# Attention: how the softmax shift rows are turned, and which score bank a maximum takes

## The reference

```
q = (x @ Wq.T + bq).reshape(b, l, H, HD).transpose(0, 2, 1, 3)
k = (x @ Wk.T + bk).reshape(b, l, H, HD).transpose(0, 2, 1, 3)
...
q = _apply_rope(q, cos, sin)
k = _apply_rope(k, cos, sin)
scores = jnp.einsum('bhsd,bhed->bhse', q, k) * scale
attn = jax.nn.softmax(scores, axis=-1)
out = jnp.einsum('bhse,bhed->bhsd', attn, v)
```

## Time and profile before

| | |
|---|---|
| time of the runs | 1195.78 us median of 3 (1195.12 to 1197.62) |
| the profiled execution | span 1191.5 us; its own whole time is not recorded |
| around the span, by the median | 4.3 us |
| TensorE busy | 1039.4 us, 87% |
| VectorE busy | 853.0 us, 72% |
| ScalarE busy | 798.2 us, 67% |
| GpSimd busy | 291.2 us, 24% |
| granted TensorE clock | 0.934 on average, 1.00 between 450 and 1020 us |

### The profile page before, as it was taken

One profiled execution on the slowest core, in us unless ns is written; L12 is line 12 of the kernel. 1 busy time (PEld: TensorE's weight loads), 2 busy tenths in 40 slices (PEclk: granted clock), 3 DMA queues, 4 the chain that ended last, 5 costly groups with the idle time before them and its releaser, 6 DMA issues.

```text
span 1191.5 us, 22203 instructions
## 1 busy us (share of the span) xinstructions
PE 1039.4 (87%) x8296; PEld 485.1 (41%) x8300; DVE 853.0 (72%) x1585; ACT 798.2 (67%) x1206; POOL 291.2 (24%) x296
## 2 busy tenths in 40 slices
PE   9936767787989689999999999999999999968795
PEld 6512224786964222222222222222222222448694
DVE  2499997347135689999999999999999992362222
ACT  2653333455545469999999999999999999431122
POOL 0069881655334500000000000000000000026652
PEclk7969998889888879999999999999999999988997
DMA  3056530866642310011100111001110100038683
GB/s 104 1 166 195 179 122 36 260 189 201 186 136 88 122 61 25 12 34 34 34 16 20 34 34 34 9 27 34 34 34 2 33 4 4 4 126 266 204 268 124
DMA packets 49110, 104.16 MB, mean 87 GB/s; under 512 B 9440, under 2 KB 11864, under 8 KB 48620
## 3 DMA queue, kind: packets, MB, share of 16 engines
q1 hardware_dynamic: 43386, 91.76, 24.6%
q0 software_dynamic: 4544, 9.32, 2.4%
q10 hardware_dynamic: 1074, 1.67, 0.4%
HBM read 89.35 MB, written 12.94 MB: 86 GB/s over the span
## 4 chain that ended last, share of the span: by engine, by line
PE 61%; issue 12%; DVE 9%; ACT 9%; DMA 4%; POOL 2%; another core or an unknown queue 1%; SPq 1%; ACTq 0%; DVEq 0%; POOLq 0%
PE psum L966 19%; PE psum L945 12%; PE psum L956 8%; PE psum L1085 6%; PE psum L1096 6%; ACT probs L1339 5%; DVE tile_max L2044 2%; DVE ssm_h L1764 1%; PE psum L789 1%; PE psum L1068 1%; PE psum L769 1%; DMA y_in<-y_dram 1%; ACT ln_xn L1331 1%; POOL h0T L1483 1%
## 5 line engine op out<-in xcount | busy, mean ns | idle before, releaser
L1339 ACT ACTIVATE probs<-psum 128x1024 f32<-128x1024 f32 x512 | 504.2, 1041 | 27.6 <-PE psum L956 22.3
L2044 DVE TENSOR_REDUCE tile_max<-psum 128x1 f32<-128x512 f32 x720 | 459.8, 685 | 31.8 <-PE psum L945 25.1
L945 PE MATMUL psum<-k_stack,q_stack 62*128 62x512 bf16 x994 | 313.3, 388 | 14.1 <-DMA q_stack<-q_dram 8.6
L966 PE MATMUL psum<-probs,v_head 128*32 128x256 f32 (+1 forms) x3840 | 321.0, 406 | 0.6 <-ACT probs L1339 0.4
L956 PE MATMUL psum<-q_stack,k_stack 64*128 64x512 bf16 x1024 | 290.0, 384 | 10.6 <-ACT probs L1339 8.7
L945 PEld LDWEIGHTS psum<-k_stack,q_stack 62*128 62x128 bf16 x994 | 77.4, 94 | 242.7 <-issue 109.7
L966 PEld LDWEIGHTS psum<-probs,v_head 128*32 128x32 f32 x3840 | 75.7, 108 | 164.6 <-issue 126.0
L1535 POOL TENSOR_TENSOR max_parts<-row_max,no_shift 128x8 bf16<-128x8 f32 x32 | 6.4, 200 | 557.0 <-DVE row_max L2020 557.0
L1096 PE MATMUL psum<-w2r,hid 128*128 128x128 f32 x624 | 92.5, 296 | 25.4 <-issue 25.2
L1085 PE MATMUL psum<-x_cols,w1r 128*128 128x128 f32 (+1 forms) x624 | 93.5, 299 | 8.8 <-issue 8.0
L1096 PEld LDWEIGHTS psum<-w2r,hid 128*128 128x128 f32 x624 | 84.3, 210 | 28.0 <-issue 27.6
(11 more groups left out here) (287 smaller groups left out, 1107.5 us busy)
## 6 DMA issues: line engine op xcount, KB each, us to landing
w1r<-w SPq DMA_DIRECT2D x78, 256.0 KB
w2r<-w SPq DMA_DIRECT2D x78, 256.0 KB
ssm_b<-bc_dram SPq DMA_DIRECT2D x32, 512.0 KB, 4.0
k_stack<-k_dram SPq DMA_DIRECT2D x60, 120.0 KB
y_in<-y_dram SPq DMA_DIRECT2D x16, 256.0 KB, 5.1
q_stack<-q_dram SPq DMA_DIRECT2D x30, 96.0 KB
bc_p<-bc_dram SPq DMA_DIRECT2D x5, 512.0 KB, 5.7
xtok_dram<-x_tok SPq DMA_DIRECT2D x8, 256.0 KB, 2.4
```

The source lines that it names most:

```text
L945: mm(bank, queries, k_stack[rows, u, keys:keys + C], start=True, stop=True).then_inc(s1_ps, 1)
L966: i = mm(psum[32 * j:32 * j + VM, 7, lo:hi], v_head[:, u, kt, :], probs[:, kt % 4, j * C + lo:j * C + hi], start=kt == 0, stop=kt == KT - ...
L1339: f(probs[:, kt % 4, hf * HALF:(hf + 1) * HALF], banks(2 * slot, 2), ACT.Exp, scale=SCALE).then_inc(p_ready, 1)
L2044: v.tensor_reduce(top, bank, AX.X, ALU.max).then_inc(s1_read, 1)
```

## The change

Part one: `row` leaves TensorE and ScalarE. `max_parts` becomes a view of `max_squares`, 32 columns for each half of which 16 are used and the rest cleared once by GpSimd. VectorE turns it in four squares of 32 partitions by 32 columns, from partitions 0, 32, 64 and 96 into `shift_rows` at partition 0 (`turn_maxima`). The turn of a half stands after VectorE's maximum 36 of the same head and after maximum 2 of the next one (`TURN_AFTER`). The row loads wait for the squares. A head has 32 entries, and the slots alternate by half tile throughout. Part two: `bank_of` takes the head itself, not its number in the ring of four stacks.

```
-WIDES = [3, 9]
-PADS = 6
+WIDES = [3, 10]
+PADS = 7
...
-ROWS_AFTER = (8, 14)
-FIRST_ROW = SN // 2 + 12
+TURN_AFTER = (SN // 2 + 4, 2)
...
+SQUARE = 32
 ROW_LOADS = 16 * 2
+SQUARES = 128 // SQUARE
...
-    return 4 + (hs % UN + p) % RING if hs else FIRST_BANKS[p % len(FIRST_BANKS)]
+    return 4 + (hs + p) % RING if hs else FIRST_BANKS[p % len(FIRST_BANKS)]
...
-ENTRIES = 2 * KT + 2
-def entry(kt, hf, rows=True):
-    return 2 * kt + hf + (rows and sum(kt > after for after in ROWS_AFTER))
-ROW = [entry(after, 1) + 1 for after in ROWS_AFTER]
+ENTRIES = 2 * KT
+def entry(kt, hf):
+    return 2 * kt + hf
...
-        max_parts = sb("max_parts", [128, 2, 2, SHIFT, TPC], BF16)
+        max_squares = sb("max_squares", [128, 2, SQUARE], BF16)
+        max_parts = max_squares[:, :, 0:ROWS].rearrange("p h (d s j) -> p h d s j", d=2, s=SHIFT)
...
-        def load_rows(eng, h, u, hf, done):
-            eng.wait_ge(p_ready, done)
+        def load_rows(eng, h, u, hf):
+
+            eng.wait_ge(max_turned, SQUARES * (2 * h + hf + 1))
...
-                        if following and kt in ROWS_AFTER:
-                            hf = ROWS_AFTER.index(kt)
-                            row(h + 1, hf, h * ENTRIES + (2 + ROW[hf]), ROW[hf] % 2)
...
+                g.memset(max_squares[:], 0.0).then_inc(pool_made, 1)
...
-                        pool.wait_ge(s2_ps, hs * ENTRIES + (2 - ENTRIES))
+                        pool.wait_ge(max_turned, SQUARES * (n - 2))
...
+                def turn_maxima(hs, hf):
+                    dve.wait_ge(max_parts_ready, hs * 4 + (hf * 2 + 4))
+                    if hs:
+                        dve.wait_ge(rows_in[hf], hs * ROW_LOADS)
+                    for g in range(SQUARES):
+                        at = slice(SQUARE * g, SQUARE * (g + 1))
+                        v.transpose(shift_rows[0:SQUARE, hf, at], max_squares[at, hf, :]).then_inc(max_turned, 1)
...
+                        if p == TURN_AFTER[0]:
+                            turn_maxima(hs, 0)
+                        if p == TURN_AFTER[1] and hs:
+                            turn_maxima(hs - 1, 1)
...
+                turn_maxima(NH - 1, 1)
```

More of the change, by code:

```diff
@@ L509, in build @@
         apart_step, above_ready = sem("apart_step"), sem("above_ready")
-        row_max_ready, max_hi_ready, max_parts_ready = (sem(n) for n in ("row_max_ready", "max_hi_ready", "max_parts_ready"))
+        row_max_ready, max_parts_ready = sem("row_max_ready"), sem("max_parts_ready")
+        max_turned = sem("max_turned")
         rows_in = [sem(f"rows_in{hf}") for hf in range(2)]
@@ L669, in attention @@
                 load_k(sp, 1, 1)
[L670 removed]
+                load_rows(sp, 0, 0, 0)
                 load_q(sp, 2, 2)
@@ L945, in maxima @@
                     mm(bank, queries, k_stack[rows, u, keys:keys + C], start=True, stop=True).then_inc(s1_ps, 1)
[L947 to L952, removed]
                 def scores(u, kt, hf, slot, side):
@@ L957, in scores, with values @@
                               q_stack[rows, u, hf * C:(hf + 1) * C], start=True, stop=True)
-                def values(h, u, kt, rows, part=None):
+                def values(h, u, kt, part=None):
                     if kt == 0:
@@ L962, in values @@
                         pe.wait_ge(o_copied, h + 1)
-                    pe.wait_ge(p_ready, h * ENTRIES + (entry(kt, 1, rows) + 5))
+                    pe.wait_ge(p_ready, h * ENTRIES + (entry(kt, 1) + 3))
                     lo, hi = (0, C) if part is None else (part * C // 2, (part + 1) * C // 2)
@@ L1009, in attention @@
                         pe.wait_ge(v_all_ready, TILES)
-                    if p == FIRST_ROW:
-                        row(0, 0, 0, 0)
                     maxima(0, 0, p)
-                for p in range(RING):
-                    maxima(1, 1, p)
-                row(0, 1, 1, 1)
-                for p in range(RING, 2 * LEAD):
+                for p in range(2 * LEAD):
                     maxima(1, 1, p)
@@ L1316, in attention @@
                 first_q(act, 0, (0,))
-                def row(hs, hf, g, slot):
-                    act.wait_ge(s2_ps, g + 1)
-                    if hs:
-                        act.wait_ge(rows_in[hf], hs * ROW_LOADS)
-                    f(shift_rows[0:ROWS, hf, :], psum[0:ROWS, 2 * slot, 0:128], ACT.Identity).then_inc(p_ready, 1)
                 def above(hs, p):
@@ L1352, in attention @@
                 above(1, 0)
-                row(0, 1, 1, 1)
-                load_rows(act, 0, 0, 1, 4)
+                load_rows(act, 0, 0, 1)
                 for h in range(NH):
-                    following = h + 1 < NH
                     for kt in range(KT):
@@ L1361, in attention @@
                         for hf in range(2):
-                            exponentials(h, kt, hf, following)
+                            exponentials(h, kt, hf)
                         if kt == 0 and h:
                             keep(h - 1)
-                        if following and kt in ROWS_AFTER:
-                            hf = ROWS_AFTER.index(kt)
-                            row(h + 1, hf, h * ENTRIES + (2 + ROW[hf]), ROW[hf] % 2)
                 keep(NH - 1)
```

38 lines of the change are left out of this document (19 added, 19 removed).

## The result

The changed kernel takes 1196.37 us (median of 20 runs) against 1190.68 us of the kernel before (20 runs beside them): ratio 1.0049, 95% interval 1.0031 to 1.0067. By this ratio it is **slower by half a per cent, 5.8 us** (3.7 to 8.0), where 0.8 us less was forecast. Its profiled execution spans 1192.3 us.

A forecast was written before the change was run, and what follows sets the result against it. TensorE was taken to set the pace, VectorE and ScalarE close behind. Terms -20.4 - 2.7 + 20.6 + 1.7 = -0.8 us, added to 1195.78, gave 1195.0 us; own range 1192 to 1198.5, whole range 1184 to 1200.

The forecast's parts named there:

- What bounds the kernel, and no slack at the joined maximum: TensorE sets the pace; a VectorE delay before the joined maximum reaches it whole, rests of 0.25 us a block recover afterwards.
- Rows out: Heads 0 to 14: two rows each leave TensorE and ScalarE, 30 x 0.68 = -20.4 us.
- the rotation: Bank clash at the ends of heads 3, 7 and 11 disappears: 3 x 0.90 = -2.7 us.
- The turns on VectorE: Four squares before a joined maximum, 29 turns on the path at 0.71 us: +20.6 us, bounds 10.4 and 27.8.
- rival B: At the joined maximum behind each turn: squares dearer than 0.19 us, TensorE waits for VectorE; 1202.6 us at upper bound, chance 0.13.
- The sum with that estimate: Whole-kernel total if each VectorE square takes the 211 ns estimated from the skill's transpose figure: 1197.9 us.
- The start: Head 0's first rows: VectorE waits for GpSimd's parts, rows issue at 427.90 instead of 426.23: +1.7 us.
- Row DMAs in time: Row loads behind VectorE's count in SP's queue still arrive before the scores; slack 0.66 us in an ordinary head, no cost.
- A (squares overlap): In each VectorE turn squares overlap, a turn is 0.36 us and the joined maximum keeps its overlap; 1184.2 us, chance 0.27.
- C: Rows miss a head's second half tile and TensorE waits once a head, 3 us per 0.2 missed; 1198.0 us, chance 0.05.
- D: The 0.68 us stall behind a row is VectorE's rest, so removing rows wins nothing; 1215.4 us, chance 0.02.
- Edits costed at nothing: GpSimd's extra memset of 64 columns, 0.06 us covered by its wait, and row DMAs unchanged in number and queue place.

The follow-up runs named there:

- the first experiment: Changed kernel with four more squares behind each turn's four, all reading partitions 0 to 31: a head takes 38.66 us, against 37.89 in the changed kernel.
- the addition later: Changed kernel with GpSimd's bias addition to xT moved behind head 0's parts, removing VectorE's wait: start 22.37 us, against 27.14 in the changed kernel.
- all four edits: Changed kernel with one instruction a turn, first turn behind maximum 41, bias addition behind head 0's parts, head 0's row loads first on SP: ratio 0.9766 to before.
- the five runs: Five timed runs of the kernel with all four edits: median 1162.73 us, ratio 0.9766 (0.9741 to 0.979) to the kernel before.
- the single run: The earlier, single execution of the kernel with all four edits: 1168.04 us beside 1192.14.

## Why the prediction was wrong

Between the forecast of 0.8 us less and the 7.7 more of the two traces lie 8.5 us: 5.9 in the turns, 2.2 in the start, 0.45 at the last head. That 1196.37 us is close to the forecast of 1195.0 is luck: the 1195.78 of three runs it was added to lies 5.1 above the median of all 20 (1190.68), and the change was put 6.5 too low (by the medians). The 4.3 us around the span were too much as well; every run with both figures has 1.8 to 1.9 (1194.07 - 1192.3).

*What bounds the kernel, and no slack at the joined maximum.* Right. A turn of 0.82 to the reduce and 0.06 of lost overlap make 0.88, and TensorE loses 0.92; the 0.04 between I can't place. Nothing of the turn was taken up. Spread over rests, half of it was.

*Rows out, -20.4, and the rotation, -2.7.* The rotation is shown by itself, 2.77. The rows' 0.68 was not measured by itself, but what rests on it agrees: 0.915 a turn from the head against 0.92 from TensorE's two half tiles, and the 3.86 us from the first rows to the last copy.

*The turns on VectorE, +20.6: this step failed, in size.* The mechanism was the one taken: the squares and the joined maximum are held, shown by the four squares from one quadrant, which were not. But I let each square begin when the one before it ends and gave it the 0.18 of a 128x32 instruction; it lasts 0.20, and a held one begins 0.03 after that end: 0.23, three times. The last square's distance to the reduce, put at 0.09, is 0.82 - 3 x 0.23 = 0.13, and what a turn makes TensorE lose is 0.92. Turn 0.915, not 0.71: 26.5 us, not 20.6, near the upper bound of 27.8 worked out from two instructions in which one waits for the other, 0.22. Those rows were the nearer ones: a held square starts 0.23 behind the one before it, about as an instruction that waits for its forerunner, not 0.18 or 0.09 like one that merely follows it. By this rival B holds, with its condition (a turn above 0.74, heads over 37.8) met and a chance of 0.13 given. What it gave as a reason, that a square must be filled before it is emptied, is not what the turn paid for: squares of one quadrant start 0.10 apart.

The Trainium skill (page VectorE: DVE Perf Modes, section Two Vector instructions with no wait between them) named the held ones rightly: the second to fourth square and the joined maximum behind, in the changed kernel; the first of the four more, but not its followers, in the first experiment. Its word on when a held one starts is that every earlier one has finished; here that is the end shown in the trace and 0.03 to 0.04 more. The Trainium skill (same page, section The three transpose paths) led to an estimate of 211 ns a square, and the trace has 0.20. The sum with that estimate, 2.1 us more than before (1197.9), has the right sign and is nearer to the 5.8 measured than the forecast's 0.8 less.

*The start, +1.7: too low, 3.87.* Row_max was forecast 0.95 later and came 1.59 later: the turn took 0.93 where 0.63 was put in, and the 14 joined maxima (420.46 - 411.50 = 8.96) 0.64 each instead of 0.61. The issue is 2.44 later, forecast 1.67. The last 1.43 was not in the sum at all: I kept the landing of the row load at its old length. The landing varies: it took 6.16 to 7.12 us in the runs of VectorE's turns with the loads of heads 2 and 3 where the changed kernel has them, and 5.69 in the kernel before (5.96 with the rotation alone). With SP's loads of heads 2 and 3 held it was 5.05, with both row loads ahead of them on SP at most 3.3. Taking away the wait or the long landing, either alone, wins the start back: without the wait it is 22.37, with the rows first 23.18, before 23.27.

*Row DMAs in time.* Right in the ordinary heads, which all last the same. Not in the last one, where TensorE waits 0.36 for them and some 0.45 us is lost. The last turn was left out of the sum because VectorE has nothing else to do there, but its rows are on the path: SP issues them at 994.99, 32.26 us behind the copy of head 13 into o_sb (962.73), before at 993.04, 32.03 behind it (961.01). So they come 0.23 later, and TensorE, freed of two rows, wants them some 0.45 sooner (two rows of 0.68 less, one turn of 0.915 more).

*The rivals.* A (squares overlap) is out: it would hold only for squares that read from one quadrant. C is seen only at the last head, once and not in each. D is out: with two turns of one instruction each a head takes 36.28, near the 36.06 that the rows' removal should leave. *Edits costed at nothing:* GpSimd's memset shows nowhere in the sums.

## What to carry to other kernels

Count the quadrants (groups of 32 partitions) that neighbouring VectorE instructions read: four small instructions on four quadrants cost 0.92 us where one over all 128 partitions costs 0.11 to 0.13, and an idle engine can bring the pieces together. Before a wait is put on a busy engine, look what stands ahead on the engine that it waits for (here an addition of 5.45 us that nobody needed yet). A DMA on the path need not keep its old landing time when it is issued later: here it landed sooner when it stood ahead of the prefetches, on the same queue.

## What the runs showed that was not expected

A VectorE transpose of 128x32 lasts 0.202 us (median of 32), a square of 32x32 0.200 when held and 0.156 when not: with 32 columns each, 128 partitions take no longer than 32. A small row load took 6.16 to 7.12 us from issue to use beside prefetches of two heads, and at most 3.3 ahead of them. The granted clock falls in head 0's second half with and without the long wait, to the lower level (1.2 GHz), where a matmul of 0.39 us takes 0.63. In the changed kernel it is 0.50 from 412 to 417 us, behind a stretch of 5 us in which TensorE was busy for 0.82 us. With the addition later it is 0.57 from 414 to 418, behind 4 us in which TensorE was busy for 3.23 us. The kernel before has it too, 0.57 from 416 to 420. With all four edits it does not fall there: it is 1.00 from 408 to 416 in the trace of the five runs (row_max of the halves at 407.04 and 417.26) and 1.00 from 412 to 420 in that of the single run (413.53 and 423.67). What brings it down was not settled.
